# The first layer's group statistics of the next image, taken inside the image before it

## The reference

```python
g = v.reshape(B_, 16, C_ // 16, H_, W_)                    # 16 groups of 2 channels
v = (g - mean(g)) / sqrt(var(g) + 1e-5)                    # one mean and variance per image and group
x_q = clip(round(v / 0.05)); w_q = clip(round(weight / 0.01))
acc = conv3x3(x_q, w_q, padding=1)                         # 32 -> 32 channels
out = clip(round((acc * 0.0005 + bias) / 0.1)) * 0.1
x = x + out
```

## Time and profile before

| | |
|---|---|
| median of three runs | 5598.68 us |
| the profiled execution's own time | 5597.51 us |
| its span, first to last instruction | 5595.8 us |
| mean granted TensorE clock | 0.967 |
| TensorE busy | 5111.7 us (91% of the span) |
| VectorE busy | 4613.7 us (82%) |
| ScalarE busy | 4026.4 us (72%) |
| first layer's matmuls (L508) | 2002.2 us, 9168 recorded |

### The profile page before, as it was taken

How to read it: one execution, slowest core, us unless ns; L and a number is a source line. 1 busy time by engine, 2 the same in 40 slices (tenths; PEclk the granted TensorE clock), 3 DMA queues, 4 the chain that set the end, 5 groups by cost and what they waited for, 6 DMA issues and landing times.

```text
span 5595.8 us, 110144 instructions
## 1 busy us (share of the span) xinstructions
PE 5111.7 (91%) x43848; PEld 3713.1 (66%) x43848; DVE 4613.7 (82%) x5393; ACT 4026.4 (72%) x2541; POOL 1164.8 (21%) x1323
## 2 busy tenths in 40 slices
PE   0989898989898989499999899999899899899899
PEld 0434343434343434289889799889799799799898
DVE  6889898989898976788788788788688788788786
ACT  1767676767676767378788688688688788788786
POOL 0000000000000000233333233233233233333233
PEclk9999999999999999799999999999999999999999
DMA  7979797979797955699999999999999999999997
GB/s 288 364 291 393 288 398 280 405 276 405 280 405 278 403 223 233 159 186 183 190 187 175 198 172 177 201 178 180 186 182 170 200 173 182 192 182 181 196 171 119
DMA packets 796691, 1333.32 MB, mean 238 GB/s; under 512 B 61080, under 2 KB 585880, under 8 KB 718952
## 3 DMA queue, kind: packets, MB, share of 16 engines
q0 software_dynamic: 185888, 539.06, 41.7%
q1 hardware_dynamic: 585232, 599.40, 37.6%
q10 hardware_dynamic: 25024, 187.38, 10.1%
HBM read 786.73 MB, written 538.84 MB: 237 GB/s over the span
## 4 chain that ended last, share of the span: by engine, by line
PE 47%; DMA 6%; SPq 2%; DVE 2%; issue 1%; ACT 1%; ACTq 0%; POOL 0%; DVEq 0%; POOLq 0%
PE c_tps L1214 35%; DMA c_x<-out_dram 6%; PE c_cps L1193 4%; PE c_cps L1194 4%; PE c_cps L1195 4%; SPq L860 2%; DVE c_z L1116 0%; ACT c_z L1075 0%; ACT c_feat L1089 0%; DVE c_feat L1147 0%; ACTq L959 0%; DVE s_gs_half L265 0%; ACT c_xr L1102 0%; DVE c_feat L1150 0%; DVE rstd L1173 0%
## 5 line engine op out<-in xcount | busy, mean ns | idle before, releaser
L1214 PE MATMUL c_tps<-c_feat,c_tt 123*128 123x256 f16 (+1 forms) x20736 | 2395.7, 274 | 103.0 <-ACT c_xr L1102 91.7
L1214 PEld LDWEIGHTS c_tps<-c_feat,c_tt 123*128 123x128 f16 (+1 forms) x20736 | 2003.6, 98 | 368.4 <-issue 102.2
L508 PE MATMUL b_ps<-b_xq,w0main 128*128 128x512 bf16 x9168 | 2002.2, 381 | 150.1 <-ACT b_haloq L442 150.1
L508 PEld LDWEIGHTS b_ps<-b_xq,w0main 128*128 128x128 bf16 x9168 | 891.5, 97 | 1255.8 <-ACT b_haloq L442 131.1
L1031 POOL DMA_DIRECT2D out_dram<-c_xr x1152 | 1057.6, 1054 | 2128.2 <-DVE c_xr L1162 1677.2
L1075 ACT ACTIVATE c_z<-c_x,c_rs 128x976 f16<-128x976 f32 x576 | 1151.0, 1999 | 165.8 <-DMA c_x<-out_dram 165.8
L1116 DVE SCALAR_TENSOR_TENSOR c_z<-c_x,c_rs,c_z 128x976 f16<-128x976 f32 x576 | 1104.4, 1918 | 126.2 <-ACT c_z L1075 106.0
L1162 DVE TENSOR_SCALAR c_xr<-c_tps 57x1024 f32<-57x1024 f32 (+1 forms) x576 | 701.1, 1217 | 479.4 <-PE c_tps L1214 433.5
L450 ACT ACTIVATE b_q<-b_ps,q_bias 128x1024 int8<-128x1024 f32 x512 | 567.3, 1110 | 599.8 <-PE b_ps L508 570.5
L1102 ACT ACTIVATE c_xr<-c_tps 57x1024 f32<-57x1024 f32 (+1 forms) x576 | 638.7, 1109 | 421.5 <-PE c_tps L1214 401.1
L1089 ACT ACTIVATE c_feat<-c_cps 122x1024 f16<-122x1024 f32 x576 | 822.8, 1429 | 155.6 <-PE c_cps L1195 123.6
(11 more groups left out here) (146 smaller groups left out, 1446.9 us busy)
## 6 DMA issues: line engine op xcount, KB each, us to landing
out_dram<-b_x POOLq DMA_DIRECT2D x128, 2048.0 KB, 8.1
out_dram<-c_xr POOLq DMA_DIRECT2D x576, 384.0 KB, 7.6
c_x<-out_dram SPq DMA_DIRECT2D x220, 912.0 KB, 21.0
b_stream<-in_x_dram SPq DMA_DIRECT2D x168, 1024.0 KB, 9.8
b_x<-in_x_dram ACTq DMA_DIRECT2D x138, 1024.0 KB, 9.1
b_x<-in_x_dram SPq DMA_DIRECT2D x138, 1024.0 KB, 8.8
out_dram<-c_xr POOLq DMA_DIRECT2D x512, 72.0 KB, 8.8
c_tt<-table_scratch ACTq DMA_DIRECT2D x56, 576.0 KB
```

Source lines behind the costliest of these rows:

```text
L508: last = pe.matmul(ps[:, g % 3, j, :], k.w0main[:, y, d, :, :].rearrange("p o r -> p (o r)"), row(2 * i + j + y - 1)[:, d:d + W], start=(y ...
L1214: last = pe.matmul(tps[:, s % 2, o % 4, :], tt[0:rows, o, tp, 2 * d:2 * d + 2, :].rearrange("k w m -> k (w m)"), feat[0:rows, (e * N + i) ...
```

## The change

Five things are changed, all in the first layer.

- TensorE does the first small product behind group 60 and the second behind group 62, both inside chunk 15, instead of both behind group 63.
- VectorE does `gs.vector_variance` right behind `gs.vector_spread`, ahead of chunk 14's statistics, and `new_scales` ahead of chunk 15's additions.
- ScalarE does the square root between the rounding of groups 62 and 63. Behind group 63 it does `round_x`, `widen_x` and `halo` of the next image's chunk 0, at the end of the loop body instead of at the start of the next. (Of the two branches in the text, `early` and `late`, `late` is the one that holds with these constants: `STAGE` is 14, so `STAGE + 3 < N + 1` is false.) The first image's are ahead of the loop. The last of ScalarE's load issues of an image is now behind this work.
- Group 63 has slot 1 of `b_ps` instead of slot 0, and so waits for the rounding of group 61. Group 0 of the next image waits only for group 60 of the one before, group 1 for all of them.
- `out_rounded` starts 3 higher, so that this can be written with constants above zero.

```diff
-    def tensor(self, pe, t):
-        for i, rhs in enumerate((self.own_mean, self.spread)):
+    def tensor(self, pe, t, parts=(0, 1)):
+        for i in parts:
+            rhs = (self.own_mean, self.spread)[i]
...
+        STAGE = N - X_SLOTS + 3 + RESIDENT - 1
+        RING = 3
...
+        def ps_slot(g):
+            return 1 if g == G * N - 1 else g % RING
...
-            def widen_x(b, n):
+            def widen_x(b, n, first=False):
                 act.wait_ge(rounded, b * N + n + 1 + START)
-                act.wait_ge(conv_done, b * (G * N) + max(0, G * (n - XQ_SLOTS + 1) + 1) + START)
+                act.wait_ge(conv_done, b * (G * N) + (max(0, G * (n - XQ_SLOTS + 1) + 1) if n or first else G * (1 - XQ_SLOTS) + 1) + START)
...
-            def halo(b, h, n):
+            def halo(b, h, n, first=False):
-                act.wait_ge(conv_done, b * (G * N) + START)
+                act.wait_ge(conv_done, b * (G * N) + (0 if h or first else 1 - G * N) + START)
...
+            def next_image(b):
+                widen_x(b + 1, 0)
+                halo(b + 1, 0, 0)
+
             def body(b, more):
                 for n in range(N + 2):
                     load_ahead(act, b, n + X_SLOTS - 5, more, 1)
-                    if n < N:
+                    early = more and n == N + 1 and STAGE + 3 < N + 1
+                    late = more and n == N + 1 and not early
+                    if early:
+                        round_x(b + 1, 0)
+                    if 1 <= n < N:
                         round_x(b, n)
...
                     if n >= 2:
                         round_out(b, n - 2, 2)
+                        if more and n == STAGE + 3:
+                            gs.scalar(act, b + 1)
                         round_out(b, n - 2, 3)
+                    if late:
+                        round_x(b + 1, 0)
+                        next_image(b)
                 load_ahead(act, b, N + AHEAD - 1, more, 1)
-                if more:
-                    gs.scalar(act, b + 1)
...
             act.wait_ge(first_read, N - AHEAD + START)
+            act.sem_inc(out_rounded, RING)
             gs.scalar(act, 0)
+            round_x(0, 0)
+            widen_x(0, 0, True)
+            halo(0, 0, 0, True)
...
-                        pe.wait_ge(out_rounded, b * (G * N) + max(0, g - 2) + START)
+                        freed = g - 1 if g == G * N - 1 else 0 if g == 1 else g - 2 if g else -RING
+                        pe.wait_ge(out_rounded, b * (G * N) + freed + RING + START)
...
                         last.then_inc(conv_done, 1)
-                if more:
-                    gs.tensor(pe, b + 1)
+                        if more and n == STAGE + 1 and i in (0, 2):
+                            gs.tensor(pe, b + 1, (i // 2,))
...
-                    if more and n == N - 2:
+                    if more and n == STAGE:
                         last.then_inc(all_taken, 1)
                         dve.wait_ge(all_taken, b + 1 + START)
                         dve.memset(gate[:, :], 0.0)
                         means(b + 1)
+                    if more and n == STAGE + 1:
+                        new_scales(b + 1)
                     for h in range(2):
                         g = 2 * n + h
-                        dve.wait_ge(out_rounded, b * (G * N) + 2 * g + 2 + START)
+                        dve.wait_ge(out_rounded, b * (G * N) + 2 * g + 2 + RING + START)
...
-                    if more and n == N - 2:
+                    if more and n == STAGE:
                         gs.vector_spread(dve, b + 1, mv_x)
-                    if more and n == N - 1:
-                        new_scales(b + 1)
+                        gs.vector_variance(dve, b + 1)
...
-                    if more and n == N - 2:
-                        gs.vector_variance(dve, b + 1)
```

More of the change, by code:

```diff
@@ L449, in round_out @@
                     act.wait_ge(added, b * (2 * N) + max(0, g // 2 - 1) + START)
-                act.activation(q8[:, i // 2, 2 * (i % 2):2 * (i % 2) + 2, :], ps[:, g % 3, :, :], ACT.Identity,
+                act.activation(q8[:, i // 2, 2 * (i % 2):2 * (i % 2) + 2, :], ps[:, ps_slot(g), :, :], ACT.Identity,
                                bias=k.q_bias[:, :], scale=S_X * S_W / S_OUT).then_inc(out_rounded, 1)
+            def next_image(b):
+                widen_x(b + 1, 0)
+                halo(b + 1, 0, 0)
             def body(b, more):
@@ L460, in body @@
                         round_out(b, n - 2, 1)
-                    if n < N:
+                    if 1 <= n < N:
                         widen_x(b, n)
-                    if n == 0:
-                        halo(b, 0, n)
+                    if early:
+                        next_image(b)
                     if n == 8:
@@ L507, in body @@
                                 for d in range(3):
-                                    last = pe.matmul(ps[:, g % 3, j, :], k.w0main[:, y, d, :, :].rearrange("p o r -> p (o r)"),
+                                    last = pe.matmul(ps[:, ps_slot(g), j, :], k.w0main[:, y, d, :, :].rearrange("p o r -> p (o r)"),
                                                      row(2 * i + j + y - 1)[:, d:d + W], start=(y == 1 and d == 0), stop=(y == 2 and d == 2))
                         last.then_inc(conv_done, 1)
-                if more:
-                    gs.tensor(pe, b + 1)
+                        if more and n == STAGE + 1 and i in (0, 2):
+                            gs.tensor(pe, b + 1, (i // 2,))
             gs.tensor(pe, 0)
```

## The result

The changed kernel takes 5565.82 us (median of four runs, 5563.66 to 5566.82) against 5598.02 for the kernel before: a ratio of 0.9944, with a 95% interval of [0.9928, 0.996]. It is 32 us faster. The forecast was 58 us, 5540, with a range that ended at 5560; the result lies outside it, and just over half of the gain came.

A forecast was written before the change was run, and what follows sets the result against it. The first layer was taken as bound by TensorE's work (91% busy) plus seven passages between images. 7 x 8.66 - 2.1 = 58.5 us less than 5597.5 gave 5540 us, range 5526 to 5560.

The forecast's parts named there:

- The chain up to the restart: Passage between images, from small products to TensorE's restart: restart at 391.92 instead of 400.58, 8.66 us less in each of seven.
- The jump: ScalarE's return to its loop top, now between halo and chunk 1: 0.35 us in six passages, 2.1 us; ends 0 and 4.2.
- The cover: Behind the restart, before TensorE's group 3 needs group 0 rounded: 2.1 us of room to hide ScalarE's return to its loop top.
- The clock: TensorE behind the passage: granted 0.50 (1.2 GHz) for 4.9 us as before, so no gain from the shorter gap.
- VectorE's lag: Behind the restart VectorE enters the new image 4.5 us later against TensorE; 1.0 us of room left, so it costs nothing.
- the lag: Rival: VectorE can't catch up in the full DMA stretch, so each image gains only 4.2 us; 5568 us, chance 0.11.
- the late mean: Rival: the own mean comes late, so TensorE stops behind group 60; slower, 5610 us, chance 0.05.
- B: Theory for the experiments, from the first rival: VectorE, late behind the restart, holds the new image back; 5568 us, chance 0.11.

The follow-up runs named there:

- VectorE's order alone: Kernel before, with only the variance moved right behind the spread and the scales ahead of chunk 15's additions: 5573.36 us, ratio 0.9945.
- jump ahead of the quantising: Changed kernel, with the next image's first quantise, widen and halo back at the top of ScalarE's loop: 5555.85 us, ratio 0.9919.
- products' place alone: Kernel before, with only the two small products moved behind groups 60 and 62: 5562.27 us, ratio 0.9936.
- turned: Changed kernel, with the end of ScalarE's loop moved between its steps n = 9 and n = 10: 5549.41 us; on another chip 5537.99 us.
- the better order: Changed kernel, ScalarE's loop end moved between n = 9 and n = 10, variance back behind chunk 14's statistics: 5524.17 us, ratio 0.9871.

## Why the prediction was wrong

**The chain up to the restart: right.** Products between groups at 0.28 us, variance, statistics, scales, restart: 8.55 us per passage measured, 8.66 forecast.

**The jump: the step that failed.** The term of the sum for ScalarE's jump was 0 to 0.7 us in each of six passages, 2.1 us in all, from VectorE's 2.83 us as the upper end. It measured 3.06 to 4.33 us: the stops at group 3 are 4.33, 3.06, 3.91, 3.83, 3.59 and 3.61 us, 22.3 in all, because the jump took 5.0 to 5.3 us. The cover that I had worked out, 2.1 us, was about right; ScalarE's idle time is 32.5 us in the six, 10.2 more than the stops, so it was 1.7 on average.

I had said that the trace does not show ScalarE's jump. It does, in the rows of L477 above, and it was 2.5 us there. With that the term would have been no larger. So what failed is not the choice of VectorE's jump in place of ScalarE's own. It is that a jump's length in one place was taken for its length in another:

| jump, kernel | branch to next instruction, us | DMA share in it, passage at 380 us |
|---|---|---|
| VectorE, changed kernel | 2.7 to 3.0 | 0.01 |
| ScalarE, before | 2.4 to 2.7 | 0.53 |
| ScalarE, VectorE's order alone | 4.5 to 5.2 | 0.51 |
| ScalarE, changed kernel | 5.0 to 5.3 | 1.03 |
| ScalarE, jump ahead of the quantising | 5.3 to 5.6 | 0.97 |
| ScalarE, products' place alone | 6.7 to 6.8 | 0.98 |
| ScalarE, turned, mid-image (at 515.8 us) | 0.20 to 0.23 | 0.91 |

Two of these shares, as windows of the trace (ScalarE busy, TensorE's granted clock, DMA share, GB/s), for the changed kernel and for the kernel before:

```profile
389.20:394.10 4.90, 0.00 (x0) 0.66 1.03 411
```

```profile
385.80:388.20 2.40, 0.00 (x0) 0.50 0.53 215
```

The rule of the Trainium skill on taken branches ("Runtime: NRT & Kernel Launch", Instruction fetch mechanics), that one to a page outside the two-page window waits for a DMA fetch of it, pointed the right way, and the traces agree. I gave a fetch too small a price. In the first window the DMA queue that brings instructions moves one packet (queue, packets, MB, share):

```profile
q14 instruction: 1, 0.01, 0.4%
```

Every jump of over 2 us in the table has such a packet, and the next instruction follows 1.5 to 2.0 us after the packet began; the jumps of 0.2 us have none on this queue. The long jumps stand where the DMA is full, but 4.6 us at a share of 0.51 is out of line, and no run changes the load around a jump alone. That the load makes them long is likely and not shown; nor does a run show that a shorter body would jump faster.

The idle time that hid the jump, 5.60 us, would have been a safer end for the term: 5.60 less the cover is 3.5, 21 us in six passages, and 5560 would not have been the end of the range.

**The clock: right once, missed once.** The slow start behind the passage came as forecast. That an exposed stop would bring a second one was no term of my sum. TensorE's windows over the six passages show it in five of them, 5.9 us once (407.0 to 412.9) and 3.4 us in four, about 20 us in all, of which half is lost, 10 us. Against it the first slow starts are shorter and give back about 3 us in all.

These make up the result: 60 (seven times 8.55) - 22 - 10 + 3 = 31. From the first restart to the layer's last matmul the traces are 31.8 us apart (2162.8 and 2131.0). The whole profiled executions are 30.7 apart (5597.51 and 5566.82): the first image starts 1.9 us earlier, which no term of mine had, and the unchanged second layer takes 3.0 longer.

**VectorE's lag: right in size, wrong as harmless.** It enters 4.5 us later and catches up in the changed kernel, which hardly waits for the stream (0.3 us in all), as the stops give TensorE's lead back. Without the stops the same lag becomes waits for the stream and, in some passages, for the own mean. Two of the prediction's rivals, the lag and the late mean, so turned out to be one chain of causes in the turned kernel; neither explains the time of the changed kernel, and B's price of 5568 us met the result by accident.

## What to carry to other kernels

When work is moved across the end of a hardware loop, the jump moves against it, and it need not keep its length: ScalarE's was 2.5 us where it was hidden, 5.0 to 6.8 where it was not, and 0.2 in the middle of an image. The rows of the loop's own line in the source show it, even where the idle time does not. A stop of a few us on TensorE can cost more than its length, since the clock may fall again. And when a stop is removed, look at who had used it to catch up: here VectorE and a DMA at 400 GB/s.

## What was not expected of the hardware

That one and the same jump takes from 0.2 to 6.8 us was not expected; what sets its length was not tried. Nor does the length of TensorE's stop alone tell whether the clock falls. In the changed kernel the stop of 3.06 us in the second passage was not followed by a low granted clock, and those of 3.59 us and more were. But without ScalarE's loop a stop of 2.82 us was followed by one, 0.52 from 1435.6 to 1439.0. And the low clock behind a restart varied from 2.7 to 6.1 us in the better order, whose stops before it are all 10.2 to 10.3 us.
